# Soft products between the two early down tiles in the first pass of a fused attention and expert layer

## The reference

```python
x = x + tanh(g_xattn) * attention(layernorm(x), ctx, wq, wk, wv, wo)
h = layernorm(x)                                    # 2048 tokens x 512
scores = softmax(h @ gate_w.T)                      # 64 experts, 8 groups of 8
w_e = top8 of scores, zero elsewhere
flat = w_e[:, inv_map]; scalar = flat.sum(-1)       # one per token and group
soft = softmax(where(flat == 0, -1e9, flat))        # inside each group
xg = h[:, None] + einsum('ngi,ghi->ngh', soft, mask_up_w)
g, u = xg @ gate_proj_w, xg @ up_proj_w             # per group, 352 wide
d = einsum('ngi,ghi->ngh', silu(g) * u, down_proj_w)
x = x + tanh(g_ffn) * einsum('ng,ngh->nh', scalar, d)
```

## Time and profile before

| | us |
|---|---|
| median of 3 runs | 1057.75 |
| lowest and highest | 1057.20 and 1058.01 |
| the profiled execution | 1059.39 |
| its span, first to last instruction | 1057.6 |
| TensorE busy | 1047.7 (99%), 5428 matmuls |
| VectorE busy | 748.4 (71%) |
| GpSimd busy | 616.6 (58%) |
| ScalarE busy | 390.9 (37%) |

### The profile page before, as it was taken

How to read it: one execution, slowest core, us unless ns; L and a number is a source line. 1 busy time by engine, 2 the same in 40 slices (tenths; PEclk the granted TensorE clock), 3 DMA queues, 4 the chain that set the end, 5 groups by cost and what they waited for, 6 DMA issues and landing times.

```text
span 1057.6 us, 14596 instructions
## 1 busy us (share of the span) xinstructions
PE 1047.7 (99%) x5428; PEld 894.7 (85%) x5428; DVE 748.4 (71%) x1315; ACT 390.9 (37%) x651; POOL 616.6 (58%) x546
## 2 busy tenths in 40 slices
PE   9999999999999999999999999999999999999998
PEld 9989989998988788878888878888888888888887
DVE  7874655676678788788789998766566566565565
ACT  5333324334434434243335333333333333332331
POOL 2012102122435976768788978768777677677661
PEclk9999999999999999999999999999999999999999
DMA  9212225255786315124223552683321220221202
GB/s 324 86 41 100 61 50 150 65 130 147 239 245 210 116 36 55 68 77 36 91 86 111 86 137 92 216 257 115 115 75 48 76 74 29 75 75 48 75 27 80
DMA packets 114341, 111.66 MB, mean 106 GB/s; under 512 B 20960, under 2 KB 96736, under 8 KB 114272
## 3 DMA queue, kind: packets, MB, share of 16 engines
q1 hardware_dynamic: 113840, 110.58, 35.9%
q10 hardware_dynamic: 432, 0.17, 0.1%
HBM read 79.07 MB, written 31.65 MB: 105 GB/s over the span
## 4 chain that ended last, share of the span: by engine, by line
PE 89%; DVE 7%; DMA 1%; issue 1%; SPq 1%; ACT 0%; POOL 0%; DVEq 0%; POOLq 0%
PE bank L85 37%; PE bank L1729 33%; PE bank L1540 9%; PE bank L1735 3%; PE bank L1559 2%; PE bank L1743 2%; DMA x2t<-x2l 1%; DVE tmp L1376 1%; DVE a_stack L1367 1%; PE bank L1714 1%; PE bank L1611 1%; DVE a_stack L1365 1%; DVE a_tmp L1359 1%; SPq L484 1%; DVE tmp L1402 1%
## 5 line engine op out<-in xcount | busy, mean ns | idle before, releaser
L1729 PE MATMUL bank<-x2t,wgu_hi 128*128 128x512 f32 x1144 | 353.0, 390 | 0.0
L672 POOL TENSOR_TENSOR wgu_lo<-wgu_raw,wgu_hi 128x768 fp32r<-128x768 f32 (+2 forms) x143 | 221.8, 1558 | 87.2 <-ACT wgu_hi L825 84.7
L1729 PEld LDWEIGHTS bank<-x2t,wgu_hi 128*128 128x128 f32 x1144 | 214.9, 188 | 44.3
L1729 PE MATMUL bank<-x2t,wgu_lo 128*128 128x512 f32 x572 | 224.2, 392 | 1.2 <-DVE tmp L1434 0.8
L825 ACT CAST wgu_hi<-wgu_raw 128x512 fp32r<-128x512 f32 (+1 forms) x129 | 93.8, 728 | 223.5 <-PE bank L1735 186.2
L1383 DVE TENSOR_TENSOR xres<-xres,bank 128x512 f32<-128x512 f32 x175 | 119.6, 683 | 47.7 <-PE bank L85 47.2
L85 PE MATMUL bank<-wd_hi,at_second 128*128 128x512 f32 x336 | 130.8, 389 | 0.0
L1729 PEld LDWEIGHTS bank<-x2t,wgu_lo 128*128 128x128 f32 x572 | 107.4, 188 | 24.4 <-issue 2.4
L644 POOL TENSOR_TENSOR kt_lo<-ctxt_raw,kt_hi 128x256 fp32r<-128x256 f32 x32 | 23.4, 762 | 136.8 <-ACT kt_hi L833 136.8
L85 PE MATMUL bank<-wd_hi,at_first 128*128 128x512 f32 x256 | 99.8, 390 | 0.4 <-DVE xres L1383 0.4
L1376 DVE TENSOR_TENSOR tmp<-tmp,scalars 128x512 f32<-128x512 f32 x88 | 89.6, 1018 | 4.4 <-DMA scalars<-scals 1.4
(11 more groups left out here) (222 smaller groups left out, 2270.0 us busy)
## 6 DMA issues: line engine op xcount, KB each, us to landing
wgu_raw<-in_w_gate_up SPq DMA_DIRECT2D x43, 512.0 KB, 4.1
wd_raw<-in_w_down SPq DMA_DIRECT2D x22, 512.0 KB, 5.1
a_stacks<-a_stack SPq DMA_DIRECT2D x22, 192.0 KB, 1.9
a_stack<-a_stacks SPq DMA_DIRECT2D x22, 192.0 KB, 3.9
ctxt_raw<-in_ctx_t SPq DMA_DIRECT2D x8, 512.0 KB, 11.4
ctx_raw<-in_ctx SPq DMA_DIRECT2D x8, 512.0 KB, 8.5
x<-x_raw SPq DMA_DIRECT2D x8, 512.0 KB, 7.8
sums_raw<-x SPq DMA_DIRECT2D x16, 256.0 KB, 3.6
```

Source lines behind the costliest of these rows:

```text
L672: last = nc.gpsimd.tensor_tensor(wgu_lo[:, part], raw_of(quad)[:, part], f32(wgu_hi[:, part]), ALU.subtract)
L1729: last = nc.tensor.matmul(out_bank[:], stationary, moving, start=begins and n == 0, stop=n == len(pairs) - 1, skip_group_check=True)
```

## The change

A new function says for which quads it holds: those with two early tiles in the first half of the quads, which is q = 3 to 21, 19 quads. There TensorE takes the two soft products after the first early down tile and ahead of the second. VectorE adds the first early tile between its sum on bank B and its sum on bank C; the other addition stays where it was. No instruction is added or taken away.

```diff
+def soft_between(q):
+
+    return early_tiles(q) == 2 and q < QUADS // 2
...
@@ VectorE, per quad
                     for t in range(ST):
                         residual(B - 1, t, first=6)
+                if soft_between(q):
+                    add_down(below)
                 dve.wait_ge(s_s3, q + 1)
                 dve.wait_ge(s_m5, q + 1)
                 nc.vector.tensor_tensor(sums[:, SUM_3], sums[:, SUM_3], psum_c[:], ALU.add).then_inc(s_c22, 1)
...
-                for n in range(early):
+                for n in range(1 if soft_between(q) else 0, early):
                     add_down(below + n)
...
@@ TensorE, per quad
                 product_7(quad)
-                soft_products(quad)
+                if not soft_between(q):
+                    soft_products(quad)
                 for n in range(early):
+                    if n == 1 and soft_between(q):
+                        soft_products(quad)
```

## The result

The changed kernel takes 1060.49 us, median of 8 runs (1059.68 to 1061.59), against 1057.80 us before (8 runs, 1057.11 to 1058.01): ratio 1.0023, interval 1.0013 to 1.0032. It is slower by 2.7 us where 3.6 us of gain were forecast, and lies outside the stated range of 1053.3 to 1056.3.

The account below looks back on a forecast made before the run. TensorE's stream bounds the kernel, held at the soft products for `a_stack`. 4.0 us of holds less 0.2 left in quad 17 and 0.2 for transfers gives 3.6 us gain: 1054.2 us, range 1053.3 to 1056.3.

Parts of the forecast that it names:

- seven holds at the soft products: TensorE waits for `a_stack` in quads 3, 4, 6, 8, 12, 16, 17: 3.25 us plus 0.75 for restarts, 4.0 together.
- VectorE's order: VectorE's sum on bank C now stands behind a wait for the first down tile: cost 0.
- GpSimd's slip: Group B on GpSimd starts later behind ScalarE's delayed SiLU and copy: 0.85 us in quad 15, at most 1.37 in any.
- rival C: Slower: GpSimd's low part C misses `masked_products` if the slip is twice 1.37 us; +2.4 us, 1060.1, chance 0.04.
- ScalarE and GpSimd: SiLU, group B's copy and GpSimd's work start later, within the slack: cost 0, at most some 0.3 in two quads.
- the line on the first down tile: First down tile right behind `product_7`: its activations and down weights come early enough; cost 0, up to 0.2 once.
- signs of being wrong: TensorE waiting for `wgu_lo`, at a first down tile for `wd_lo` or `at_lo`, or at `product_4` for bank B's sum.
- VectorE had slack at exactly this place.: VectorE waited for down tiles 38 times, 18.9 us, 0.5 each, so its new wait there costs 0.
- A: GpSimd's slip is handed to VectorE's `a_stack` chain through the shared memory: gain only 1.9 us, 1055.8, chance 0.13.
- B: Holds are VectorE's backlog and return at `product_4` or the second down tile: time stays 1057.7, chance 0.08.
- The exclusive lock: VectorE's two-input SBUF instructions and GpSimd's SBUF reads block each other; in quad 17, 1.41 and 2.05 us against 0.55.
- The transfers: SyncE's burst of second-pass token loads slips by 0.66 us, mostly absorbed: cost between 0 and 0.66, taken as 0.2.

Follow-up runs that it names:

- copy_first: The changed kernel with ScalarE copying weight group B ahead of SiLU in quads 3 to 21: 1054.77 us, ratio 0.9968 to the kernel before.
- dve_only: The kernel before with only VectorE's part of the change, TensorE's order as before: 1058.00 us, ratio 1.0000.
- not_q20: The changed kernel without the change in quad 20: 1060.11 us, ratio 1.0020 to the kernel before.
- pe_only: The changed kernel with VectorE's order as before, so TensorE's part alone: 1060.20 us, ratio 1.0019 to the kernel before.
- copy_first_alone: The kernel before, soft products unmoved, with ScalarE copying weight group B ahead of SiLU in quads 3 to 21: 1059.93 us, ratio 1.0018.
- late_b: The kernel before with ScalarE's copy of group B also waiting for the first early down tile in quads 3 to 21: 1060.81 us, ratio 1.0026.

## Why the prediction was wrong

**What held.** The bound was read rightly: TensorE's stream, seven holds at the soft products, 4.0 us with the restarts. They went as forecast. The 4.0 is 0.5 too much for a forecast of the median, though, since quad 3's hold was one of the profiled execution alone; `copy_first` gains 3.4 us. VectorE's order costs nothing (`dve_only`). GpSimd's slip was right in size where it was worked out: in quad 15 group B starts 3.4 us behind `product_7`, before 2.6, so 0.8 where 0.85 was said. Low part C still meets `masked_products` in every quad (rival C); its slack in quad 16 fell to 0.60 us, as worked out. In other quads the slip was larger than the 1.37 us that the prediction gave as its most: low part C ends 0.66 to 1.94 us later against `masked_products`.

**The step that failed** is "ScalarE and GpSimd", with its "Cost 0, at most some 0.3 in two quads". I priced the slip by who waits for GpSimd's results. In the first pass hardly anybody waits for them too long. The price is paid by who shares the memory with GpSimd: VectorE's scale (L1376), its routing steps and its low parts of the token sums (L1387) came to run beside other GpSimd instructions, so that VectorE enters the next quad up to 1.2 us late. Its measure is 4.84 us of holds at `product_5`, at down tiles and at routing work. Where the prediction did look at this tie, it looked at `a_tile` alone, which the move had just given 1.37 us of cover, and it read quad 17, the longest chain, as the worst place; the losses came in quads 14, 16, 18 and 20 and in the routing quads, ahead of `a_tile`. The same step made the line on the first down tile wrong ("Cost 0, up to 0.2 once"): it was held by 0.94 us in four quads, for low down weights that were late behind VectorE, one of the signs of being wrong that the prediction lists.

**"VectorE had slack at exactly this place."** It had, at the down tiles. That slack is not there at the mask: in quads 4, 5, 8 and 9 the mask was already 0.8 to 1.1 us behind the masked matmuls before the change, and the mean over quads 4 to 20 went from 0.26 to 0.71 us. I had read VectorE's waits where it waits, not its distance where it is waited for.

**The rivals.** A named the mechanism, but for `a_stack` only and at 2.1 us with the transfers; it was more than twice that, elsewhere. B, that TensorE's stops come back elsewhere, is nearest in effect, but its reason is wrong: the stops are not the same backlog, since with the copy ahead of SiLU they don't return. That the kernel would be slower had a chance of 0.04, and for a reason (C) that did not come.

**The exclusive lock.** The lock that the Trainium skill states (SBUF — State Buffer, "SBUF: two separate sides") is borne out beyond quad 17: the scale takes 0.69 us free and 1.67 under a GpSimd low part, ending 0.55 us after it. The prediction set L1359's 1.41 us against the free L1367; a free L1359 takes 0.29 (128x128), so its lengthening was larger than it looked. The rule was applied to `a_tile` alone; what the change moved were VectorE's other instructions on SBUF.

**The transfers.** The slip of the burst was put at 0.66 us and measured 1.29 (0.46 to 1.75 us behind quad 21's first product), since low part C of quad 21 slipped by more than quad 15's. Its price was put at 0.2 us; quad 22 took 1.17 us more (17.75 for 16.58), with a second hold. The term was mis-sized, and it carries somewhat under half of the loss. `not_q20` shows that an early start does not do away with it; what decides it stays open.

## What to carry to other kernels

Moving an instruction on the engine that sets the time also moves all that stands behind its reader in that reader's queue. Follow that queue to the end, and ask of each shifted instruction not only who waits for its result but what it will now run beside; where VectorE and GpSimd both work from on-chip memory, a slip of 1 us can lengthen one instruction more in each round, as it did here. Then look whether the shifted part can be taken out of the queue: here one swap on ScalarE turned +2.7 us into -3.4.

## What was not expected of the hardware

Kernels that give the engines the same order show nearly the same collisions from execution to execution (in quads 3 to 21 the mask's lateness agrees between `pe_only` and the changed kernel to 0.02 us, with TensorE 0.7 us apart by the clock), so here the phase between two engines is mostly a property of the program, and an edit elsewhere changed VectorE's busy time by 13 us through it. Quad 3 of the kernel before is the exception. The burst of token transfers, in contrast, ends up to 1.9 us apart with the same start. And GpSimd early is no safer than GpSimd late: in the kernel before, group B started 0.5 us earlier in the median (`copy_first_alone`) cost 1.8 us, and 0.8 us later (`late_b`) cost 2.6.
